# Two gathered tables moved from SyncE's queue to GpSimd's indirect DMAs, one chunk sent whole by SyncE, and x split ahead of the first chunk

## The reference, cut to what matters

```
# layer 0: gated FFN with LoRA (16 adapters, rank 16), then a product with sign(weight)
gate = x @ W_gate.T + 0.5 * (x @ A_gate[id0].T) @ B_gate[id0].T
up   = x @ W_up.T   + 0.5 * (x @ A_up[id0].T)   @ B_up[id0].T
act  = silu(gate) * up
down = act @ W_down.T + 0.5 * (act @ A_down[id0].T) @ B_down[id0].T
x    = x + down @ sign(weight).T + bias0
# layer 1: LoRA of 64 adapters, rank 16, then W plus eight weighted LoRA products
h = (x @ B[id1].T) @ A[id1].T
x = x + h @ (W + 2 * sum_n w_n * lora_B[n] @ lora_A[n]).T + bias1
```

## Time and profile before

| | |
|---|---|
| median of three runs | 961.37 us (961.15 to 965.55) |
| the profiled execution | 962.87 us |
| its span | 959.9 us |
| mean granted clock of TensorE | 0.998 |
| PE busy | 928.4 us (97%) |
| DVE, ACT, POOL busy | 422.8, 170.2, 93.2 us (44%, 18%, 10%) |
| DMA, mean over the span | 141 GB/s |

### The profile page before, as it was taken

How to read it: one execution, slowest core, us unless ns; L and a number is a source line. 1 busy time by engine, 2 the same in 40 slices (tenths; PEclk the granted TensorE clock), 3 DMA queues, 4 the chain that set the end, 5 groups by cost and what they waited for, 6 DMA issues and landing times.

```text
span 959.9 us, 28224 instructions
## 1 busy us (share of the span) xinstructions
PE 928.4 (97%) x10528; PEld 708.2 (74%) x10528; DVE 422.8 (44%) x1051; ACT 170.2 (18%) x318; POOL 93.2 (10%) x81
## 2 busy tenths in 40 slices
PE   9999999999999999999999999999999999999988
PEld 6887786777777777777777777777777777777765
DVE  5754343444434344344434444434344344434434
ACT  6731111111111111101111110111111111111101
POOL 0300110111001001110110111011011100100111
PEclk9999999999999999999999999999999999999999
DMA  9934444445454454544544454454454545444442
GB/s 349 366 98 115 139 126 117 139 139 143 121 143 135 118 138 132 145 130 130 145 121 125 139 142 136 126 143 127 124 139 134 143 122 141 135 123 135 136 111 66
DMA packets 166679, 135.23 MB, mean 141 GB/s; under 512 B 55681, under 2 KB 138369, under 8 KB 166529
## 3 DMA queue, kind: packets, MB, share of 16 engines
q1 hardware_dynamic: 102640, 105.15, 37.7%
q10 hardware_dynamic: 63072, 26.64, 10.7%
q0 software_dynamic: 944, 3.15, 0.8%
HBM read 92.11 MB, written 11.01 MB: 107 GB/s over the span
## 4 chain that ended last, share of the span: by engine, by line
PE 95%; issue 3%; DMA 1%; DVE 0%; ACT 0%; ACTq 0%; SPq 0%
PE gu_ps L786 52%; PE y_ps L830 27%; PE gu_ps L919 3%; PE out_ps L850 3%; PE out_ps L887 2%; PE y_ps L786 1%; PE out_ps L839 1%; PE out_ps L786 1%; PE gu_ps L910 1%; PE out_ps L860 1%; PE gu_ps L959 0%; DMA landed<-act_sb 0%; DMA lb_raw<-in_lbw 0%; PE gu_ps L1031 0%; ACTq L242 0%
## 5 line engine op out<-in xcount | busy, mean ns | idle before, releaser
L830 PE MATMUL y_ps<-down_sb,actT_sb 128*128 128x512 f32 x1056 | 267.1, 401 | 13.8 <-issue 13.7
L786 PE MATMUL gu_ps<-wu_sb,xT_sb 128*128 128x512 f32 (+1 forms) x1152 | 256.6, 369 | 7.1 <-issue 7.1
L830 PEld LDWEIGHTS y_ps<-down_sb,actT_sb 128*128 128x128 f32 x1056 | 192.0, 189 | 89.8 <-issue 39.8
L786 PE MATMUL gu_ps<-wg_sb,xT_sb 128*128 128x512 f32 (+1 forms) x1152 | 256.0, 371 | 1.5 <-DVE xT_sb L577 1.5
L786 PEld LDWEIGHTS gu_ps<-wg_sb,xT_sb 128*128 128x128 f32 x1152 | 204.3, 188 | 56.9 <-DVE xT_sb L577 27.8
L786 PEld LDWEIGHTS gu_ps<-wu_sb,xT_sb 128*128 128x128 f32 x1152 | 204.7, 188 | 44.0 <-issue 16.1
L577 DVE TENSOR_TENSOR actT_sb<-landed,actT_sb 128x512 fp32r<-128x512 f32 (+1 forms) x96 | 62.2, 648 | 221.9 <-ACT actT_sb L431 220.9
L431 ACT CAST actT_sb<-landed 128x512 fp32r<-128x512 f32 (+1 forms) x96 | 56.1, 585 | 414.7 <-DMA landed<-act_sb 288.7
L597 DVE TENSOR_TENSOR act_sb<-act_sb,gu_ps 128x512 f32<-128x512 f32 (+1 forms) x94 | 58.1, 618 | 125.4 <-ACT act_sb L444 125.4
L444 ACT ACTIVATE act_sb<-gu_ps 128x512 f32<-128x512 f32 (+1 forms) x96 | 49.6, 551 | 329.3 <-PE gu_ps L910 300.8
L620 DVE STREAM_TRANSPOSE lhs_sb<-t_own 32x32 f32<-32x32 f32 x512 | 103.9, 203 | 7.7
(11 more groups left out here) (135 smaller groups left out, 424.6 us busy)
## 6 DMA issues: line engine op xcount, KB each, us to landing
b_rows<-in_btab SPq DMA_DIRECT2D x128, 216.0 KB, 3.0
landed<-act_sb ACTq DMA_DIRECT2D x186, 64.0 KB, 2.2
ad_raw<-in_adtab SPq DMA_DIRECT2D x128, 88.0 KB, 2.1
xT_raw<-in_xT SPq DMA_DIRECT2D x32, 256.0 KB, 3.1
a_raw<-in_atab SPq DMA_DIRECT2D x128, 64.0 KB, 1.9
x_in<-in_x SPq DMA_DIRECT2D x32, 256.0 KB
x_landed<-x_turn ACTq DMA_DIRECT2D x124, 64.0 KB, 2.6
out_x<-out_sb SPq DMA_DIRECT2D x31, 256.0 KB, 2.4
```

The source lines that it names most:

```text
L786: last = nc.tensor.matmul(o, w, m, start=start and n == 0, stop=stop and n == len(terms) - 1, skip_group_check=not check)
L830: last = nc.tensor.matmul(y_ps[:], actT_sb[:, ACTT_SLOT[c] + n, a, :], down_sb[:, blk, b, :], start=c == begin and n == 0 and (a, b) == (0 ...
```

## The change

SP no longer loads the sb and c rows. GpSimd gathers them, with one indirect DMA for each batch row, whose 16 source rows are taken from a list of 16 row numbers in SBUF. The lists are four columns of a new table `idx_rows`, made by two more DVE instructions in the prologue, and copied ahead of each four gathers by one GpSimd instruction, which GpSimd then waits for. The gathers of both kinds come after `first_mm` of the step, between `add_bias0` and `add_bias1`. SP's `ad_raw` loads move ahead of its `b1_raw` loads. SP sends all four quarters of chunk 2, and ACT none. ACT and DVE split x of the next step ahead of chunk 0 of this one.

```diff
@@ tiles
+        idx_rows = place("idx_rows", [P, 2, BATCH], i32, line=32)
+        now_sb = place("now_sb", [P, GB], i32, line=32)
+        now_c = place("now_c", [P, GB], i32, line=32)
@@ sync
-            def load_ad_sbd(g):
-                if isinstance(g, int) and g < 2:
-                    sp.wait_ge(L["first_mm"], g + 1)
+            def load_ad(g):
                 for b in range(GB):
                     at = row_of(0, g, b, R0)
                     sp.dma_start(ad_raw[:, b, :], adtab[bass.ds(at, P), :]).then_inc(L["ad_in"], 16)
-                    sp.dma_start(cs_rows[even_rows(3, 4), b, :], sb_view[bass.ds(at, P), :].rearrange("(r e) w -> r (e w)", e=8)
-                                 ).then_inc(L["sbd_in"], 16)
-
-            def load_c(g):
-                if last(g):
-                    sp.wait_ge(L["first_mm"], g + 2)
-                for b in range(GB):
-                    at = row_of(1, g, b, R1)
-                    sp.dma_start(cs_rows[even_rows(2, 3), b, :], c_view[bass.ds(at, P), :].rearrange("(r e) w -> r (e w)", e=8)
-                                 ).then_inc(L["c_in"], 16)
@@ sync, step
-                    send_act(sp, prev, 2, range(0, 2))
+                    send_act(sp, prev, 2)
...
                 copy_lhs(g)
+                load_ad(g)
                 if prev is not None:
                     load_b1(prev)
                 if pp is not None:
                     store(pp)
-                load_ad_sbd(g)
-                if prev is not None:
-                    load_c(prev)
@@ sync, finish
-                load_c(g)
@@ gpsimd
+            def gather_rows(g, ids, now, r, table, signal):
+                nc.gpsimd.tensor_copy(now[:], idx_rows[:, ids, bass.ds(g * GB, GB)]).then_inc(L["idx"], 1)
+                pool.wait_ge(L["idx"], 1)
+                pool.sem_clear(L["idx"])
+                for b in range(GB):
+                    nc.gpsimd.indirect_dma_start(
+                        out=cs_rows[even_rows(r, r + 1), b, :], out_offset=None, in_=table,
+                        in_offset=bass.IndirectOffsetOnAxis(ap=now[0:RANK, b:b + 1], axis=0)).then_inc(signal, 16)
+
+            def step(g, prev, pp):
+                if prev is not None:
+                    add_bias0(prev)
+                pool.wait_ge(L["first_mm"], g + 1)
+                gather_rows(g, 0, now_sb, 3, sb_table, L["sbd_in"])
+                if prev is not None:
+                    gather_rows(prev, 1, now_c, 2, c_table, L["c_in"])
+                    add_bias1(prev)
...
             add_bias0(G - 1)
+            pool.wait_ge(L["first_mm"], G + 1)
+            gather_rows(G - 1, 1, now_c, 2, c_table, L["c_in"])
             pool.wait_ge(E["x1_tr"], 2)
@@ scalar, step
-                    send_act(act, prev, 2, range(2, 4))
...
-                split_actT(g, 0)
                 if nxt is not None:
                     split_xT(nxt)
+                split_actT(g, 0)
@@ vector, prologue
+                nc.vector.tensor_scalar(idx_rows[:, n, :], id_f[:, n, :], float(RANK), row_number,
                                         ALU.mult, ALU.add).then_inc(S["ids_done"], 1)
```

More of the change, by code:

```diff
@@ L193, in build_adaln_ffn @@
                  "out_done", "stored", "a_in", "ad_in", "b1_in", "b_in", "c_in", "sbd_in", "small_mm", "small_scaled",
-                 "lhs_ready", "lhs2_in", "first_mm", "second_mm", "y_mm", "silu_done", "act_done", "act_turned",
+                 "lhs_ready", "lhs2_in", "first_mm", "second_mm", "y_mm", "idx", "silu_done", "act_done", "act_turned",
                  "act_in0", "act_in1", "act_in2", "actT_hi", "actT_lo")
@@ L219, in by_row @@
             return tile.rearrange("p (r n i) -> p r n i", r=4, n=4)
-        sb_view = sb_table.rearrange("n (e w) -> (n e) w", e=P // RANK)
-        c_view = c_table.rearrange("n (e w) -> (n e) w", e=P // RANK)
         def act_in(c):
@@ L314, in load_ad_sbd @@
                     sp.dma_start(ad_raw[:, b, :], adtab[bass.ds(at, P), :]).then_inc(L["ad_in"], 16)
-                    sp.dma_start(cs_rows[even_rows(3, 4), b, :], sb_view[bass.ds(at, P), :].rearrange("(r e) w -> r (e w)", e=8)
-                                 ).then_inc(L["sbd_in"], 16)
-            def load_c(g):
-                if last(g):
-                    sp.wait_ge(L["first_mm"], g + 2)
-                for b in range(GB):
-                    at = row_of(1, g, b, R1)
-                    sp.dma_start(cs_rows[even_rows(2, 3), b, :], c_view[bass.ds(at, P), :].rearrange("(r e) w -> r (e w)", e=8)
-                                 ).then_inc(L["c_in"], 16)
-            sp.wait_ge(S["ids_done"], 2)
+            sp.wait_ge(S["ids_done"], 4)
             load_a(0)
@@ L417, in _ @@
             pool.wait_ge(S["bias_in"], 16)
[L418 to L422, removed]
+            step(0, None, None)
+            step(1, 0, None)
+            step(2, 1, 0)
+            with pool.Fori(3, G - 1) as g:
+                step(g, g - 1, g - 2)
+            step(G - 1, G - 2, G - 3)
             add_bias0(G - 1)
+            pool.wait_ge(L["first_mm"], G + 1)
+            gather_rows(G - 1, 1, now_c, 2, c_table, L["c_in"])
             pool.wait_ge(E["x1_tr"], 2)
@@ L737, in _ @@
                 nc.vector.tensor_scalar(idx_feat[:, n, :], id_f[:, n, :], float(P), row_number,
+                                        ALU.mult, ALU.add).then_inc(S["ids_done"], 1)
+                nc.vector.tensor_scalar(idx_rows[:, n, :], id_f[:, n, :], float(RANK), row_number,
                                         ALU.mult, ALU.add).then_inc(S["ids_done"], 1)
```

## The result

| | before | after |
|---|---|---|
| median of 4 runs each, us | 963.31 (961.15 to 965.55) | 1138.09 (1127.93 to 1140.75) |
| ratio, 95% interval | | 1.1795 [1.1712, 1.1877] |
| profiled execution, us | 962.87 | 1140.75 |
| its span, us | 959.9 | 1138.9 |
| mean granted clock | 0.998 | 0.918 |

The forecast was 941.5 us, faster. The kernel became 18% slower. A, B and C are cut as in the prediction, from PE's timeline. The step is the mean of steps 2 to 30; A, B and C are means over the loop's steps, 3 to 30, here and in the table of the experiments, so they need not add up to the step to the last digit.

What follows compares the result with a forecast made beforehand. The prediction took SP's queue, not PE (busy 97%), to set the step. From 962.87 us it subtracted 19.4 (29 steps of 0.67) and 1.5 for step 1, giving 942.0, stated as 941.5; range 931 to 957.

Steps and rivals of the forecast that it cites:

- A: Part of a PE step from its first product to its narrow products; forecast at 9.51 us.
- B: Part of a PE step from the narrow products to first_rows; forecast between 6.8 and 7.7 us.
- C: Part of a PE step from first_rows to the next step; taken as unchanged at 10.5 us.
- SP's queue as the bound: Claim that SP's queue, going round without slack, sets the step of 27.77 us, not PE.
- T: The time of a step's first product on PE, from which times in the step are counted.
- Step 1's wait of 1.55 us: PE's wait for x as step 1 begins; splitting x ahead of chunk 0 was to save 1.5 us.
- A gather near 1.0 us: Assumed GpSimd cost of one indirect gather, 1.0 us, set close to a direct DMA's 0.56 us.
- The forecast step of 27.1 us: First_rows at T + 16.6 plus 10.5 us for C; saves 0.67 us a step, 19.4 us over 29.
- That is cover for 15 us.: GpSimd's gathers and add_bias1 end at T + 28, the rows are wanted at T + 43.7.
- C has no wait in it: Premise that PE's products from first_rows to the next step follow each other without a gap, 10.50 us in step 14.
- The slow rival: Slow gathers make GpSimd the bound: from 2.7 us a gather; at 3.5 us, 5.5 more a step, 1128 us; chance 0.08.
- The collision of add_bias1 with DVE's subtractions: Rival: GpSimd's moved addition shuts out DVE's subtractions, chunk 2 turns later, only 1.5 us saved, 961.4 us; chance 0.08.

Runs made afterwards that it cites:

- e5: The kernel before with chunk 2 sent whole by SP and x split ahead of chunk 0, all loads where they were; 997.1 us, ratio 1.034.
- e2: The changed kernel with the c rows loaded by SP again at the end of its step, four gathers a step left; 946.9 us against 963.8 before.
- e1: The kernel before plus GpSimd's eight gathers a step into a tile that nobody reads; 965.5 us against 963.8 before, on chip 5.
- e4: The changed kernel with GpSimd's gathers replaced by eight direct DMAs of the same rows; 955.5 us against 963.8 before, on chip 5.
- e19: e1 unchanged, run again on chip 11 in four executions; 1153.1 us against 963.0 for the kernel before, ratio 1.197.

## Why the prediction was wrong

**Right.** SP's queue as the bound (e5 shows it by itself). SP waiting for the transpose in each step (182.0 / 31 = 5.9 us each, where some 4 were forecast for a step 6.5 us shorter), the first send at T + 3.76 (3.75), x at T + 8.2 (8.25), B between 6.8 and 7.7 at the freed pace (7.24 in e2; 6.60 in the kernel after, perhaps because its loads have the hold's time to land). A of 9.5 where no hold comes (9.53 in e2). Step 1's wait of 1.55 us gone: its first product stands at 73.80, 1.70 us earlier than before. A gather near 1.0 us: 0.84, 1.15 from start to start. The forecast step of 27.1 us is nearly reached by e2 on chip 5 (27.31), with the c loads still on SP. The changed kernel itself was not run on chip 5, so whether it would reach its forecast there is open.

**The step that failed** is the one on GpSimd: "That is cover for 15 us." It charged the gathers to GpSimd's queue alone and took their price on the other queues as zero, without saying so and without a bound for it. With that went the premise "C has no wait in it". The cover was there: GpSimd was idle for most of the step, and nobody waited for its rows. The cost fell on engines that have no part in the gathers: 5.3 us a step of hold at the end of C, and through the granted clock 1.7 us a step in the next A. No row of the trace before shows an indirect DMA; what it shows, a direct DMA of GpSimd in the prologue, lies where nothing of the step's kind runs beside it.

**The rivals.** The slow rival gave 1128 us, close to the time, by a mechanism that did not occur: it needed gathers of 2.7 us and more, and GpSimd was 28% busy. A number that fits confirms nothing by itself. The collision of add_bias1 with DVE's subtractions could not show either: in the kernel after, DVE does no work while the addition runs (440.02 to 441.29). The Trainium skill (SBUF — State Buffer, "SBUF: two separate sides") says that on the engine side only the port pair shared by DVE and GpSimd causes contention, and that PE and ACT never wait on anyone. If this rule covered all that can stop an engine, PE and ACT would not have stood; in this trace they did, and SP's queue with them. So either the hold comes from something else than SBUF's ports, or the rule is not complete.

**What stays open.** What the held engines lack. PE's rows say "issue", no semaphore. PE ran some 40 more products after SP had begun to stall (from 432.72 to 438.5), and only then stood. One might think of a store of fetched instructions that runs out while their supply is cut. The trace gives no support to this as far as the supply comes by recorded transfers. The profile page of the kernel after has 14 + 8 = 22 packets of instruction queues, but the DMA view from 200 to 1050 us, where step after step is held, lists these queues only (packets, MB, share of the 16 engines):

```profile
q1 hardware_dynamic: 78832, 68.36, 28.6%
q10 hardware_dynamic: 43302, 18.09, 8.3%
q0 software_dynamic: 6528, 6.70, 3.4%
```

Full DMA engines are not the reason either: their share in the held stretch of step 11 is 0.25. And every execution here has a span and a granted clock on record, so each was recorded; whether the hold stands in one that nobody records is not shown.

Open too is why e1, e2 and e4 ran free on chip 5, in one execution each, while the eleven other kernels with eight gathers in a row, and e1's again as e19, held on chips 3, 7, 11, 15 and on that of the first comparison, whose number is not on record. And because e4 ran on chip 5 only, it doesn't show that direct DMAs from GpSimd are safe elsewhere. The changed kernel with SP's real loads put beside the gathers was not tried.

## What to carry to other kernels

An instruction new to a kernel needs two prices: its time on its own engine, and what it does to every other queue. The second is found by running it unused beside the kernel before, and, as e1 against e19 shows, in more than one execution and on more than one chip, even where the kernel before agrees to half a per cent on all of them. Of a row of indirect DMAs from GpSimd, the length of the row matters more than the count: eight in a row cost six to seven us a step (e19 against e1, after against the forecast), four and four about one. And before work is taken off a full queue, its wait table says what the relief is worth: 1.0 us of slack a step is all that e2 had, and a hold of 2.1 us turned its gain into a loss.

## What the runs showed that was not expected

- Eight indirect DMAs of 16 rows of 2 KB in a row on GpSimd held SP, ACT, DVE and in the end PE, 8.04 us for four loads of SP that take 3.04 alone. GpSimd's own pace didn't change (1.15 us).
- One program, 965.5 us on one chip (one execution) and 1151.8 to 1155.2 on another (four), with the kernel before within 0.5% on both.
- The price behind the hold: with PE at 4.05 us busy in 6, the granted clock afterwards was 0.50, and twelve products took 3.62 us in place of 2.19.
- Step 16 of the kernel after, which begins at 578.71, lasted 27.1 us, and the next 36.3. In it the fourth gather came 2.16 us after the third in place of 1.15, at 602.23. PE's narrow products ran through, and the gaps came behind them:

```profile
604.72 1.15 PE L926 MATMUL gu_ps<-b_rows,lhs_sb 32*32 32x512 f32 x32
605.81 1.56 PE L793 MATMUL gu_ps<-wg_sb,xT_sb 128*128 128x352 f32 x8
608.51 0.32 PE L793 MATMUL gu_ps<-wg_sb,xT_sb 128*128 128x352 f32 x1 [1.14 <-issue]
```

  The same pair of steps stands out in all other kernels that held (27.0 to 29.4 us, then 35.4 to 37.6), except e19 (33.7, then 34.3). I have no explanation for it.
